# Value context laid out by the host: six tiles of 125 keys and one transfer per chunk, in a cross-attention and mixture-of-experts kernel

## The chip, the core and the metric

The kernel runs on one core of a Trainium2 chip. The metric is the device time of one launch in microseconds, the median of the runs shown. A core has TensorE (matmuls), VectorE (DVE), ScalarE (ACT), GpSimd (POOL) and SyncE (SP), which here issues nearly all transfers, and sixteen DMA engines that carry them out.

## What is computed

x is 8 x 224 x 2048 in float32, the context ctx_4096 is 8 x 750 x 2048. The first half is attention, in which the context is key and value at once, the second a feed-forward layer with a low-rank top-2 mixture of sixteen experts. Cut to what matters here:

```python
def _L0_xattn_ref(query, key):
    a = jnp.einsum('bqd,bkd->bqk', query, key)
    e = jax.nn.softmax(a, axis=-1)
    c = jnp.einsum('bqk,bkd->bqd', e, key)
    return c

x = x + _L0_xattn_ref(_layernorm(x, axis=-1), ctx_4096)
x = x + _L0_ffn_ref(_layernorm(x, axis=-1), base_w, base_b, A, B, router_w)
```

## The kernel before

Each float32 product is made of three matmuls: an operand is split into a high part, converted by ACT, and a low part, which DVE makes by subtraction, and high x high, high x low and low x high are added in PSUM.

The attention half goes through the eight batches one after another (`one(b, stage)` on every engine). A batch has two phases on TensorE.

*Scores.* Queries stand as the stationary operand, two tiles (q) of QT = 112 columns. The context comes transposed (`ctxT`, laid out by the host), in eight pairs j of two 128-row blocks, 750 KB each, into LR = 4 slots. ACT's `ctx_high` (L1045) and DVE's `ctx_low` (L1287) split a pair; lines 789 to 791 multiply. Step j of the scores ends when its pair has been used; SP may load pair j + 4 then (`score_done`).

*Values.* The exponentials (`prob`) are transposed on TensorE (`exps_T`, L884), NT = 6 tiles of keys. Then `outputs_of` (L906 to 908) goes through CH = 4 chunks of 512 columns and, in each, the six tiles t. The keys of a tile are the contraction, so a tile has as many partitions as keys: 128 five times (FULL), then REST = 110. ACT's `value_high` (L1067) and DVE's `value_low` (L1297) split a tile. A chunk c is loaded by `load_raw` (L522, L524), one transfer for the five full tiles, one for the rest, both counted on `raw_loaded[c]`; its buffer is loaded again for the next batch (`raw_again`) when TensorE has used the chunk (`val_used`).

SP's queue is written out by hand in `one` of the sync block. For a batch b in the middle it issues: the late store of x2 of batch b - 1; ctxT pairs 4 to 7, each behind score step j - 4; value chunk 3; ctxT pairs 0 to 3 of batch b + 1 behind score steps 4 to 7; x rows and xT of batch b + 1; value chunk 0 of b + 1; the stores of xT and hn of batch b - 1; value chunks 1 and 2; the early store of x2. In the first batch chunks 0 to 3 are loaded between its own ctxT pairs, in the order ctxT 0 to 3, chunk 0, ctxT 4, x rows, ctxT 5, chunk 1, ctxT 6 and 7, chunk 2, ar, chunk 3, x rows of batch 1. All these transfers go through one queue of SP (q1 in the profile), which has a lane on each of the sixteen DMA engines. DVE takes the statistics of the next batch's x rows in between values 4 to 7 (`row_stats`), in program order.

Behind the eight batches comes the expert half: base weights, routing, expert rows and output tiles (L937 to 939 and others).

Of the kernel before, what the change touches and what calls it, by code (L numbers as in the profile page):

```python
# [24 lines left out]
F32 = mybir.dt.float32  # L25
# [4 lines left out]
P = 128  # L30
BANK = 512
# [6 lines left out]
def as_f32(ap):  # L38

    return ap.bitcast(F32)  # L40
# [29 lines left out]

def xattn_ffn_kernel(nc, x, ctx, bias, ctxT, xT, arT, wT, bT, out):
    NB, LQ, D = x.shape
    LK = ctx.shape[1]
    E, R = bT.shape[0], bT.shape[1]
    QT = LQ // 2
    NQ = 2
    KD = D // P
    NT = -(-LK // P)
    FULL = LK // P
    REST = LK - FULL * P  # L80
    CH = D // BANK
    RE = R + E
    assert LQ == NQ * QT and D == CH * BANK and RE <= P and 2 * R == P


    T = NB * LQ
# [57 lines left out]
    out = out.rearrange("b s d -> (b s) d")  # L144
# [59 lines left out]
    with ExitStack() as stack:  # L204
        def sb(name, shape, dt=F32, of=stack):
            return of.enter_context(nc.sbuf_tensor(name, shape, dt))
# [17 lines left out]
        ident = sb("ident", [P, P])  # L224
# [28 lines left out]
        NR = 4  # L253
        with ExitStack() as first:
            xn = sb("xn", [QT, NQ, D], F32, first)
            ctxT_l, ctxT_in = sb_in("ctxT", [P, LR, CP, LK], first)
            ctxT_h = [sb(f"ctxT_h{i}", [P, CP, LK], F32R, first) for i in range(HR)]
            prob = sb("prob", [QT, NQ, NT * P], F32, first)
            raw, raw_in = sb_in("raw", [P, CH, NT, BANK], first)
            val_h = sb("val_h", [P, NR, BANK], F32R, first)  # L260
            eT_h = sb("eT_h", [P, NQ, NT, QT], F32R, first)
            eT_l = sb("eT_l", [P, NQ, NT, QT], F32R, first)
            at_x2 = [nc.sbuf_base]
            x2 = sb("x2", [QT, NQ, D], F32, first)
# [14 lines left out]
        rows = [xn, x2]  # L279
# [5 lines left out]
        for i in range(AR):  # L285
# [3 lines left out]
            low_part, loaded = sb_in(f"a{i}", [P, KD, P], stack)  # L289
# [76 lines left out]
        consts_ready = sem("consts_ready")  # L366
# [6 lines left out]
        raw_loaded = [sem(f"raw_loaded{c}") for c in range(CH)]  # L373
# [93 lines left out]
        def xT_count(batches):  # L467
            return 16 * sum(len(pieces_of(b)) for b in range(batches))

        def rows_of(t):  # L470
            return P if t < FULL else REST

        X2T_TAIL_AT = (3, 6, 9, 12)
        HID_TAIL_AT, HN_TAIL_AT = 1, 6
        HR_AT, ROUTE_AT, COUNT_AT, PLACE_AT, SCATTER_AT = 3, 4, 6, 6, (6, 7, 8, 9)
# [42 lines left out]
        @block.sync  # L518
        def _(sp):
            def load_raw(b, c):  # L520
                cols = slice(c * BANK, (c + 1) * BANK)
                sp.dma_start(raw_in[:, c, 0:FULL, :],  # L522
                             ctx[b, 0:FULL * P, cols].rearrange("(t p) d -> p t d", p=P)).then_inc(raw_loaded[c], 16)
                sp.dma_start(raw_in[0:REST, c, FULL, :], ctx[b, FULL * P:LK, cols]).then_inc(raw_loaded[c], 16)  # L524

            def load_ctxT(b, j):
                sp.dma_start(ctxT_in[:, j % LR, :, :], ctxT[b, j]).then_inc(ctx_loaded[j % LR], 16)
# [248 lines left out]
        def _(pe):  # L776
# [100 lines left out]
            def exps_T(stage, b):  # L877
                for q in range(NQ):
                    pe.wait_ge(exp_done, b * NQ + q + 1)
                    take(job_no(stage, b, "eT", q))  # L880
                    slot = slot_of(stage, "eT", q)
                    for t in range(NT):
                        at = (t // 3) * BANK + (t % 3) * QT
                        last = pe.transpose(work[:, slot, at:at + QT],  # L884
                                            prob[:, q, t * P:(t + 1) * P], ident[0:QT, 0:QT])
                    last.then_inc(filled, 1)

            def outputs_of(stage, b):

                pe.wait_ge(drained, job_no(stage, b, "eT", NQ - 1) + 1)  # L890
                for e in range(CH * NT):
                    c, t = e // NT, e % NT
                    if stage != "first" and e == HN_AT:
                        hidden_back(stage, b)
                    if stage != "last" and e == SPREAD_AT:
                        spread_mean(stage, b)
                    if t == 0 and c >= 2:

                        pe.wait_ge(x2_done, b * (NQ * CH) + NQ * (c - 1))
                    pe.wait_ge(val_ready, b * (CH * NT) + e + 1)  # L900
                    for q in range(NQ):
                        out = scores[0:QT, (c + 1) % 2, q * BANK:(q + 1) * BANK]
                        used = rows_of(t)
                        eh, el = eT_h[0:used, q, t, :], eT_l[0:used, q, t, :]
                        vh, vl = val_h[0:used, e % NR, :], raw[0:used, c, t, :]
                        pe.matmul(out, eh, vh, start=(t == 0), stop=False)  # L906
                        pe.matmul(out, eh, vl, start=False, stop=False)  # L907
                        last = pe.matmul(out, el, vh, start=False, stop=(t == NT - 1))  # L908
                    last.then_inc(val_used, 1)
# [124 lines left out]
        def _(act):  # L1034
            def high(stage, b, name, n, out, cols, width):

                act.wait_ge(filled, job_no(stage, b, name, n) + 1)
                src = place(stage, name, n).rearrange("p (k c) -> p k c", k=cols)[:, :, 0:width]
                act.activation(out, src, ACT.Copy).then_inc(high_done, 1)

            def ctx_high(b, j):
# [19 lines left out]
            def value_high(b, e):  # L1061
                at_least(act, val_used, b * (CH * NT) + e - NR + 1)
                c, t = e // NT, e % NT
                if t == 0:
                    act.wait_ge(raw_loaded[c], b * 32 + 32)
                used = rows_of(t)
                act.activation(val_h[0:used, e % NR, :], raw_in[0:used, c, t, :],  # L1067
                               ACT.Copy).then_inc(val_high, 1)

            def exponentials(b, q):  # L1070
# [18 lines left out]
            def one(b, stage):  # L1089
# [29 lines left out]
                    high(stage, b, "x2T", NX - 1, four_blocks(nT_h, NX - 1), 2, 2 * LQ)  # L1119
                exponentials(b, 1)  # L1120
                for q in range(NQ):
                    high(stage, b, "eT", q, eT_h[:, q, :, :].rearrange("p (k i) c -> p k (i c)", k=2), 2, 3 * QT)
                for e in range(NR, CH * NT):
                    value_high(b, e)
                    if stage == "first" and e == AR_AT:
# [152 lines left out]
        def _(dve):  # L1278
            def low(stage, b, name, n, high_part, low_part, cols, width):

                dve.wait_ge(high_done, act_no(stage, b, name, n) + 1)
                src = place(stage, name, n).rearrange("p (k c) -> p k c", k=cols)[:, :, 0:width]
                dve.tensor_tensor(low_part, src, as_f32(high_part), ALU.subtract).then_inc(drained, 1)  # L1283

            def ctx_low(b, j):
# [7 lines left out]
            def value_low(b, e):  # L1293
                c, t = e // NT, e % NT
                dve.wait_ge(val_high, b * (CH * NT) + e + 1)
                used = rows_of(t)
                dve.tensor_tensor(raw[0:used, c, t, :], raw_in[0:used, c, t, :], as_f32(val_h[0:used, e % NR, :]),  # L1297
                                  ALU.subtract).then_inc(val_ready, 1)

            def stats(tile, st, sem_stat, i):  # L1300
# [145 lines left out]
            def run_route(lo, hi):  # L1446

                steps = route_steps()
                assert len(steps) == COUNTED
                if lo == 0:  # L1450
                    dve.wait_ge(hr_loaded, 16)
                    dve.wait_ge(row_ids, 2)
                    dve.wait_ge(consts_ready, 1 + E)
                for n in range(lo, hi):
                    if n > 0:
                        dve.wait_ge(route, n)
                    if n == 2:
                        dve.wait_ge(rexp_done, 1)
                    steps[n]().then_inc(route, 1)
# [39 lines left out]
            def one(b, stage):  # L1499
# [41 lines left out]
                if old:  # L1541
                    x2T_low(NX - 1)
                for q in range(NQ):
                    three = lambda tile: tile[:, q, :, :].rearrange("p (k i) c -> p k (i c)", k=2)
                    low(stage, b, "eT", q, three(eT_h), three(eT_l), 2, 3 * QT)
                if old:
                    hidden_out(stage, b)
# [111 lines left out]
                dve.tensor_copy(y_out[:, s % 3, c * BANK:(c + 1) * BANK], y_bank(c)).then_inc(y_right, 1)  # L1659

            dve.memset(part_of_D[:, :], 1.0 / D).then_inc(part_ready, 1)
            dve.memset(prob[:, :, LK:NT * P], 0.0).then_inc(consts_ready, 1)
            for e in range(E):
                dve.memset(rank[:, e:e + 1], float(E - e)).then_inc(consts_ready, 1)
            for n in range(NX):
# [16 lines left out]
            ctx_low(0, 1)  # L1682
            first_low_part(1)
            first_centre(2)
            dve.wait_ge(consts_ready, 1 + E)
            one(0, "first")
            for b in range(1, NB - 1):
                one(b, "mid")
# [251 lines left out]
```

## Time and profile before

| | us |
|---|---|
| median of 3 runs | 1351.94 |
| lowest and highest | 1350.43, 1354.08 |
| the profiled execution | 1354.39 |
| its span (first to last instruction) | 1352.6 |
| TensorE busy | 1327.3 |
| DVE, ACT, POOL busy | 974.7, 601.2, 322.5 |
| granted clock, mean of the span | 0.996 |

Busy times are sums over the span and overlap. Times within the profile count from the span's start. Line numbers are those of the kernel before.

### The profile page before, as it was taken

What the parts mean: (1) busy time and instruction counts of PE and PEld (TensorE: products, weight loads), DVE (VectorE), ACT (ScalarE), POOL (GpSimd) and SP (SyncE); (2) the same over time, 40 slices, a digit from 0 to 9 for tenths busy, and PEclk for the clock granted to TensorE, in tenths of its full rate; (3) what the DMA queues carried; (4) which work ended last, traced back from release to release, by engine and by line L of the source; (5) the groups of instructions that cost most, each with busy time, mean ns of one, the idle gap of its engine ahead of it and who ended that gap; (6) DMA issues with size and microseconds to landing.
All of it is one profiled execution on the core that took longest, in us unless ns stands there. A gap on an engine that the chain in (4) does not pass through costs nothing.

```text
span 1352.6 us, 16784 instructions
## 1 busy us (share of the span) xinstructions
PE 1327.3 (98%) x6543; PEld 1081.0 (80%) x6543; DVE 974.7 (72%) x1254; ACT 601.2 (44%) x768; POOL 322.5 (24%) x229
## 2 busy tenths in 40 slices
PE   7799999999999999999999999999999999999998
PEld 5578788887878788887888888888788888888887
DVE  5698888889798888879475467777677555465554
ACT  3356554645546464546321367877686211111110
POOL 0003012130302112120615723354442111111110
PEclk9899999999999999999999999999999999999999
DMA  9976968878796977769657598999995977878775
GB/s 326 315 258 215 294 242 242 269 251 271 227 304 212 287 259 248 246 227 194 201 161 211 176 296 288 321 324 310 315 250 192 322 255 242 281 250 263 253 260 164
DMA packets 159359, 345.67 MB, mean 256 GB/s; under 512 B 51696, under 2 KB 68080, under 8 KB 145520
## 3 DMA queue, kind: packets, MB, share of 16 engines
q1 hardware_dynamic: 140688, 277.06, 64.5%
q0 software_dynamic: 10528, 52.85, 12.6%
q10 hardware_dynamic: 8064, 14.68, 3.1%
q8 instruction: 52, 0.85, 0.3%
q14 instruction: 27, 0.22, 0.0%
HBM read 260.87 MB, written 99.41 MB: 266 GB/s over the span
## 4 chain that ended last, share of the span: by engine, by line
PE 75%; DVE 12%; DMA 5%; ACT 3%; POOL 3%; issue 2%; SPq 0%; DVEq 0%; POOLq 0%; ACTq 0%
PE scores L937 12%; PE scores L939 12%; PE scores L938 12%; PE scores L906 6%; PE scores L908 6%; PE scores L907 6%; PE scores L789 4%; PE scores L791 3%; PE scores L790 3%; DVE ctxT_l L1287 3%; PE work L973 2%; PE work L974 2%; DMA y_scratch<-y_out,yrow_i 2%; DVE raw_l L1297 2%; POOL hs_scratch L1830 2%
## 5 line engine op out<-in xcount | busy, mean ns | idle before, releaser
L937 PE MATMUL scores<-w_h,a_h 128*128 128x512 f32 x896 | 352.0, 393 | 0.0
L939 PE MATMUL scores<-w_h,a_l 128*128 128x512 f32 x896 | 350.9, 392 | 0.0
L938 PE MATMUL scores<-w_l,a_h 128*128 128x512 f32 x896 | 350.6, 391 | 0.0
L1159 ACT ACTIVATE a_h<-a_in 128x512 fp32r<-128x512 f32 x148 | 83.6, 622 | 313.4 <-DMA a_in<-xT_scratch 211.3
L939 PEld LDWEIGHTS scores<-w_h,a_l 128*128 128x128 f32 x896 | 168.4, 188 | 37.5
L937 PEld LDWEIGHTS scores<-w_h,a_h 128*128 128x128 f32 x896 | 168.3, 188 | 37.5 <-DVE w_l L1584 0.3
L938 PEld LDWEIGHTS scores<-w_l,a_h 128*128 128x128 f32 x896 | 168.5, 188 | 37.1
L1593 DVE TENSOR_TENSOR a_l<-a_in,a_h 128x512 fp32r<-128x512 f32 x148 | 106.0, 763 | 115.3 <-ACT a_h L1159 111.8
L789 PE MATMUL scores<-ctxT_h,nT_h 128*112 128x494 f32 (+1 forms) x512 | 174.3, 340 | 7.8 <-DVE nT_l L1485 7.2
L1067 ACT ACTIVATE val_h<-raw_in 128x512 fp32r<-128x512 f32 x192 | 120.2, 629 | 127.6 <-PE scores L908 127.6
L791 PE MATMUL scores<-ctxT_h,nT_l 128*112 128x494 f32 (+1 forms) x512 | 171.5, 335 | 0.0
L790 PE MATMUL scores<-ctxT_l,nT_h 128*112 128x494 f32 (+1 forms) x512 | 171.4, 335 | 0.0
L1297 DVE TENSOR_TENSOR raw_l<-raw_in,val_h 128x512 fp32r<-128x512 f32 x192 | 153.3, 824 | 22.9 <-ACT val_h L1067 22.6
L906 PE MATMUL scores<-val_h,eT_h 128*112 128x512 f32 (+1 forms) x384 | 154.7, 403 | 3.4 <-DVE eT_l L1283 1.7
L907 PE MATMUL scores<-raw_l,eT_h 128*112 128x512 f32 (+1 forms) x384 | 152.2, 396 | 0.0
L908 PE MATMUL scores<-val_h,eT_l 128*112 128x512 f32 (+1 forms) x384 | 152.1, 396 | 0.0
L1772 POOL TENSOR_TENSOR rs<-ve,mhalf 112x2 f32<-112x2 f32 x16 | 39.4, 2463 | 404.4 <-DVE ve L1310 404.4
L1045 ACT ACTIVATE ctxT_h<-ctxT_in 128x1500 fp32r<-128x1500 f32 x63 | 90.8, 1452 | 96.2 <-PE scores L791 87.7
L1287 DVE TENSOR_TENSOR ctxT_l<-ctxT_in,ctxT_h 128x1500 fp32r<-128x1500 f32 x63 | 107.6, 1717 | 35.6 <-ACT ctxT_h L1045 35.6
L1797 POOL TENSOR_TENSOR res<-res,bias_b 128x512 f32<-128x512 f32 x42 | 63.9, 1523 | 288.6 <-DMA res<-x_scratch 264.6
L1651 DVE TENSOR_TENSOR b_hl<-b_in,b_hl 64x2048 fp32r<-64x2048 f32 x43 | 99.3, 2312 | 43.3 <-ACT b_hl L1175 43.0
L789 PEld LDWEIGHTS scores<-ctxT_h,nT_h 128*112 128x112 f32 x512 | 90.1, 176 | 23.9 <-DVE nT_l L1485 8.5
(168 smaller groups left out, 1936.6 us busy)
## 6 DMA issues: line engine op xcount, KB each, us to landing
ctxT_in<-in_ctxT_dram SPq DMA_DIRECT2D x63, 750.0 KB, 4.7
raw_in<-in_ctx_dram SPq DMA_DIRECT2D x32, 1280.0 KB
a_in<-xT_scratch SPq DMA_DIRECT2D x37, 1024.0 KB
w_in<-in_wT_dram SPq DMA_DIRECT2D x32, 512.0 KB, 6.7
y_add<-y_scratch SPq DMA_DIRECT2D x56, 256.0 KB, 6.2
late_y<-y_scratch SPq DMA_DIRECT2D x56, 256.0 KB, 6.0
nT_in<-in_xT_dram SPq DMA_DIRECT2D x7, 1792.0 KB, 10.1
res<-x_scratch SPq DMA_DIRECT2D x42, 256.0 KB
```

The lines of the kernel that those rows point to most:

```text
L789: pe.matmul(out, qh, ch, start=(k == 0), stop=False)
L790: pe.matmul(out, qh, cl, start=False, stop=False)
L791: last = pe.matmul(out, ql, ch, start=False, stop=(k == KD - 1))
L906: pe.matmul(out, eh, vh, start=(t == 0), stop=False)
L907: pe.matmul(out, eh, vl, start=False, stop=False)
L908: last = pe.matmul(out, el, vh, start=False, stop=(t == NT - 1))
L937: pe.matmul(o, ah, wh, start=(k == 0), stop=False)
L938: pe.matmul(o, ah, wl, start=False, stop=False)
L939: last = pe.matmul(o, al, wh, start=False, stop=(k == KD - 1))
L1067: act.activation(val_h[0:used, e % NR, :], raw_in[0:used, c, t, :], ACT.Copy).then_inc(val_high, 1)
L1287: dve.tensor_tensor(ctxT_l[:, j % LR, :, :], ctxT_in[:, j % LR, :, :], as_f32(ctxT_h[j % HR][:, :, :]), ALU.subtract).then_inc(ctx_ready, 1)
L1297: dve.tensor_tensor(raw[0:used, c, t, :], raw_in[0:used, c, t, :], as_f32(val_h[0:used, e % NR, :]), ALU.subtract).then_inc(val_ready, 1)
```

## The change

The host cuts the values' context into `[batch, chunk, key within tile, tile, 512]` with 750 = 6 x 125. A partition of a chunk then reads 6 x 512 floats, 12 KB in one piece, from the first 125 partitions' rows, and a chunk is one transfer. FULL, REST and `rows_of` go; tiles, conversions, transposes and matmuls of the values have KT = 125 rows. `prob` shrinks from 768 to 750 columns, and the memset of its padding goes. The semaphore of a chunk counts 16 a batch instead of 32.

```diff
@@ -70,17 +70,16 @@
-    LK = ctx.shape[1]
+    LK = ctxT.shape[-1]
...
-    FULL = LK // P
-    REST = LK - FULL * P
+    KT = LK // NT
...
-            prob = sb("prob", [QT, NQ, NT * P], F32, first)
+            prob = sb("prob", [QT, NQ, LK], F32, first)
...
             def load_raw(b, c):
-                cols = slice(c * BANK, (c + 1) * BANK)
-                sp.dma_start(raw_in[:, c, 0:FULL, :],
-                             ctx[b, 0:FULL * P, cols].rearrange("(t p) d -> p t d", p=P)).then_inc(raw_loaded[c], 16)
-                sp.dma_start(raw_in[0:REST, c, FULL, :], ctx[b, FULL * P:LK, cols]).then_inc(raw_loaded[c], 16)
+                sp.dma_start(raw_in[0:KT, c, :, :], ctx[b, c]).then_inc(raw_loaded[c], 16)
...
-                        last = pe.transpose(work[:, slot, at:at + QT],
-                                            prob[:, q, t * P:(t + 1) * P], ident[0:QT, 0:QT])
+                        last = pe.transpose(work[0:KT, slot, at:at + QT],
+                                            prob[:, q, t * KT:(t + 1) * KT], ident[0:QT, 0:QT])
...
-                        used = rows_of(t)
-                        eh, el = eT_h[0:used, q, t, :], eT_l[0:used, q, t, :]
-                        vh, vl = val_h[0:used, e % NR, :], raw[0:used, c, t, :]
+                        eh, el = eT_h[0:KT, q, t, :], eT_l[0:KT, q, t, :]
+                        vh, vl = val_h[0:KT, e % NR, :], raw[0:KT, c, t, :]
...
                 if t == 0:
-                    act.wait_ge(raw_loaded[c], b * 32 + 32)
-                used = rows_of(t)
-                act.activation(val_h[0:used, e % NR, :], raw_in[0:used, c, t, :],
+                    act.wait_ge(raw_loaded[c], b * 16 + 16)
+                act.activation(val_h[0:KT, e % NR, :], raw_in[0:KT, c, t, :],
                                ACT.Copy).then_inc(val_high, 1)
...
-            dve.memset(prob[:, :, LK:NT * P], 0.0).then_inc(consts_ready, 1)
...
+    laid["ctx_4096"] = ctx.reshape(nb, -(-lk // 128), -1, d // 512, 512).transpose(0, 3, 2, 1, 4)
```

SP's queue in batch 1, from the load of xT to the first stores, before (a row names line, operation, target<-source and the shape):

```order
L549 DMA nT_in<-in_xT_dram 128x3584
L522 DMA raw_in<-in_ctx_dram 128x5x512
L524 DMA raw_in<-in_ctx_dram 110x512
L616 DMA xT_scratch<-xT_st 128x16x128
L616 DMA xT_scratch<-xT_st 128x16x96
L621 DMA hn_scratch<-hn 112x2x80
```

and the same place now:

```order
L542 DMA nT_in<-in_xT_dram 128x3584
L517 DMA raw_in<-in_ctx_dram 125x3072
L609 DMA xT_scratch<-xT_st 128x16x128
L609 DMA xT_scratch<-xT_st 128x16x96
L614 DMA hn_scratch<-hn 112x2x80
```

Two transfers have become one at the same place in the queue; nothing else has moved, on SP or on another engine.

## Rows read from the trace of the kernel before

**Rows 1.** The page: busy time of the engines; the SP queue's packets, MB, share.
```profile
PE 1327.3 (98%) x6543; PEld 1081.0 (80%) x6543; DVE 974.7 (72%) x1254; ACT 601.2 (44%) x768; POOL 322.5 (24%) x229
...
q1 hardware_dynamic: 140688, 277.06, 64.5%
```
**Rows 2.** Windows, two middle batches; columns as in the first line.
```profile
core 0: us, PE busy (x) PEld busy (x) DVE busy (x) ACT busy (x) POOL busy (x), PEclk, DMA share, GB/s
...
182.70:259.40 76.70, 76.62 (x433) 62.70 (x432) 66.10 (x85) 40.41 (x48) 14.23 (x7) 1.00 0.81 259
...
413.40:490.10 76.70, 76.57 (x434) 62.92 (x433) 66.25 (x87) 40.39 (x48) 14.39 (x7) 1.00 0.78 259
```
**Rows 3.** DMA view, 573 to 583 us: packets, queue, issues.
```profile
DMA packets 923, 2.33 MB, mean 233 GB/s; under 512 B 43, under 2 KB 43, under 8 KB 921
...
q1 hardware_dynamic: 921, 2.30, 68.0%
...
raw_in<-in_ctx_dram SPq DMA_DIRECT2D x1, 1280.0 KB
ctxT_in<-in_ctxT_dram SPq DMA_DIRECT2D x1, 750.0 KB, 4.4
raw_in<-in_ctx_dram SPq DMA_DIRECT2D x1, 220.0 KB
```
**Rows 4.** Groups by form: value matmuls, value conversions, weight load of the transposes.
```profile
L906 PE MATMUL scores<-val_h,eT_h 128*112 128x512 f32 x320 | 129.4, 404 | 2.7 <-DVE eT_l L1283 1.7 <-DVE raw_l L1297 0.7
...
L1067 ACT ACTIVATE val_h<-raw_in 128x512 fp32r<-128x512 f32 x160 | 100.0, 629 | 108.7 <-PE scores L908 108.7
...
L906 PE MATMUL scores<-val_h,eT_h 110*112 110x512 f32 x64 | 25.3, 395 | 0.7 <-DVE raw_l L1297 0.7
...
L1067 ACT ACTIVATE val_h<-raw_in 110x512 fp32r<-110x512 f32 x32 | 20.2, 632 | 18.9 <-PE scores L908 18.9
...
L884 PEld LDWEIGHTS work<-ident,prob 112*128 112x128 f32 x96 | 9.6, 140 | 2.0 <-ACT prob L1072 2.0
```
**Rows 5.** DMA view, 1 to 40 us, in 40 slices.
```profile
GB/s 40 158 368 423 415 404 403 412 434 418 425 419 418 382 388 386 389 296 91 166 425 413 235 260 252 277 353 233 240 400 368 372 386 394 291 249 362 384 387 391
...
q1 hardware_dynamic: 3799, 13.15, 97.2%
```
**Rows 6.** SP in order of time; the queue's bytes and share, 454 to 480 us.
```profile
454.44 0.47 SPq L524 DMA_DIRECT2D raw_in<-in_ctx_dram  x1
454.96 6.60 SPq L616 DMA_DIRECT2D xT_scratch<-xT_st  x2
...
q1 hardware_dynamic: 6888, 7.65, 91.2%
```
**Rows 7.** Tile ctxT_in, 480 to 500 us: conversions, issue to landing.
```profile
L1045 ACT ACTIVATE ctxT_h<-ctxT_in x4: 1456/1456/1461, 483.5 to 496.2; 128x1500 fp32r<-128x1500 f32 x4
L1287 DVE TENSOR_TENSOR ctxT_l<-ctxT_in,ctxT_h x4: 1714/1718/1722, 485.0 to 497.7; 128x1500 fp32r<-128x1500 f32 x4
...
DMA to landing us min/median/max: 4.3/4.4/5.4
```
**Rows 8.** TensorE and ACT in order of time, the loop's two ends.
```profile
453.82 0.40 PE L906 MATMUL scores<-val_h,eT_h 128*112 128x512 f32 x1
...
496.24 1.46 ACT L1045 ACTIVATE ctxT_h<-ctxT_in 128x1500 fp32r<-128x1500 f32 x1 [0.56 <-PE scores L791]
```
**Rows 9.** First batch: the chain's wait for ctxT; DVE's wait for x rows.
```profile
26.61 13.12 DMA ctxT_in<-in_ctxT_dram
...
64.35 1.29 DVE L1302 BATCH_NORM_STATS2 st<-x 112x6 f32<-112x512 f32 x2 [2.11 <-DMA x<-in_x_dram]
```
**Rows 10.** Windows, first batch: busy time, then granted clock (columns of rows 2).
```profile
33.00:57.00 24.00, 16.49 (x95) 13.17 (x94) 17.24 (x26) 10.80 (x15) 1.64 (x1) 0.99 1.04 308
57.00:63.50 6.50, 5.54 (x13) 4.06 (x14) 1.55 (x2) 0.69 (x3) 0.00 (x0) 0.50 1.00 283
```

More of the change, by code:

```diff
@@ L78, in xattn_ffn_kernel @@
     NT = -(-LK // P)
-    FULL = LK // P
-    REST = LK - FULL * P
+    KT = LK // NT
     CH = D // BANK
     RE = R + E
-    assert LQ == NQ * QT and D == CH * BANK and RE <= P and 2 * R == P
+    assert LK == NT * KT and LQ == NQ * QT and D == CH * BANK and RE <= P and 2 * R == P
     T = NB * LQ
@@ L468, in xT_count @@
             return 16 * sum(len(pieces_of(b)) for b in range(batches))
-        def rows_of(t):
-            return P if t < FULL else REST
         X2T_TAIL_AT = (3, 6, 9, 12)
@@ L1037, in high @@
                 act.wait_ge(filled, job_no(stage, b, name, n) + 1)
-                src = place(stage, name, n).rearrange("p (k c) -> p k c", k=cols)[:, :, 0:width]
+                rows = out.shape[0]
+                src = place(stage, name, n)[0:rows, :].rearrange("p (k c) -> p k c", k=cols)[:, :, 0:width]
                 act.activation(out, src, ACT.Copy).then_inc(high_done, 1)
@@ L1121, in one @@
                 for q in range(NQ):
-                    high(stage, b, "eT", q, eT_h[:, q, :, :].rearrange("p (k i) c -> p k (i c)", k=2), 2, 3 * QT)
+                    high(stage, b, "eT", q, eT_h[0:KT, q, :, :].rearrange("p (k i) c -> p k (i c)", k=2), 2, 3 * QT)
                 for e in range(NR, CH * NT):
@@ L1281, in low @@
                 dve.wait_ge(high_done, act_no(stage, b, name, n) + 1)
-                src = place(stage, name, n).rearrange("p (k c) -> p k c", k=cols)[:, :, 0:width]
+                rows = low_part.shape[0]
+                src = place(stage, name, n)[0:rows, :].rearrange("p (k c) -> p k c", k=cols)[:, :, 0:width]
                 dve.tensor_tensor(low_part, src, as_f32(high_part), ALU.subtract).then_inc(drained, 1)
@@ L1295, in value_low @@
                 dve.wait_ge(val_high, b * (CH * NT) + e + 1)
-                used = rows_of(t)
-                dve.tensor_tensor(raw[0:used, c, t, :], raw_in[0:used, c, t, :], as_f32(val_h[0:used, e % NR, :]),
+                dve.tensor_tensor(raw[0:KT, c, t, :], raw_in[0:KT, c, t, :], as_f32(val_h[0:KT, e % NR, :]),
                                   ALU.subtract).then_inc(val_ready, 1)
@@ L1452, in run_route @@
                     dve.wait_ge(row_ids, 2)
-                    dve.wait_ge(consts_ready, 1 + E)
+                    dve.wait_ge(consts_ready, E)
                 for n in range(lo, hi):
@@ L1543, in one @@
                 for q in range(NQ):
-                    three = lambda tile: tile[:, q, :, :].rearrange("p (k i) c -> p k (i c)", k=2)
+                    three = lambda tile: tile[0:KT, q, :, :].rearrange("p (k i) c -> p k (i c)", k=2)
                     low(stage, b, "eT", q, three(eT_h), three(eT_l), 2, 3 * QT)
@@ L1684, in _ @@
             first_centre(2)
-            dve.wait_ge(consts_ready, 1 + E)
+            dve.wait_ge(consts_ready, E)
             one(0, "first")
```

## The prediction

> **What bounds the kernel now.** I read the page's busy line first: TensorE is busy 98% of the span, and the SP queue's transfers take 64.5% of the sixteen DMA engines [rows 1]. Then the windows cut at batch borders: a batch of the attention half takes 76.7 us, TensorE is busy all of it, and the DMA engines stand at 0.78 to 0.81 [rows 2]. So TensorE sets the pace and the DMA has a fifth to spare, as long as the bytes lie evenly on the sixteen engines. The expert half, behind the eight batches, has none of the edited lines.
>
> **How a transfer is spread.** This decides everything, and one short window shows it. Between 573 and 583 us three transfers run: the 128-partition part of a value chunk (640 rows of 2 KB), its 110-partition rest (110 rows), and one ctxT pair (128 rows). That makes 878 data packets; the SP queue shows 921, so 43 small ones are left, and 43 is also the count under 512 B [rows 3]. If every transfer ended with one small packet on each of sixteen engines there would be 48. 43 is 16 + 16 + 11: the 110-partition transfer used eleven engines, ten partitions each. 110 does not divide by 16, and 11 is its largest factor up to 16. The new transfer has 125 partitions on both sides; 125 is 5 x 5 x 5, so the same division gives **five engines with 25 partitions each**. The Trainium skill (DMA: Bandwidth & Descriptors, Why a DMA increments its semaphore by 16 and not by 1) says that a transfer takes the largest number of engines up to 16 that divides the slowest dimension of both sides; this trace agrees with its 11. By that rule the sum is the one below; by an even spread it would be about nothing.
>
> **The change part by part.**
> Instruction shapes: values with 125 rows in place of 128 and 110. The two old forms cost the same: 404 against 395 ns a matmul, 629 against 632 ns a conversion on ACT [rows 4]; counts don't change. 0 us. The transposes of the exponentials load 125 columns in place of 128: 96 loads of about 0.14 us, by a fortieth less [rows 4], under 1 us. The removed memset on DVE runs while the first load is under way: 0. One transfer fewer per chunk takes 0.47 us off SP thirty-two times [rows 6], but SP waits for TensorE between its issues, so 0; if it did not, 15 us would be the most, and no row shows TensorE waiting for SP. Fewer, larger packets: bytes are the same, a gain I take as 0 (below).
>
> The five engines: a chunk is 125 x 12 KB = 1.536 MB. Before, each engine carried 96 KB of it; now five carry 307 KB. Price: with all sixteen busy and large packets, slices of the start-up run at 403 to 434 GB/s [rows 5], which is 25 to 27 GB/s for one engine; over the mixed first 39 us it is 13.15 MB at 97.2% busy, 21.7 GB/s for one engine [rows 5]. So a chunk takes 11.4 to 14.2 us on those five. I take 25 GB/s, **12.3 us**, because only five engines will then ask HBM. Before, it was 3.8 us by the same rate. Everything else on the queue also has a sixteenth on each of these five engines, and each engine works in order, so all later transfers wait for them.
>
> Middle batches. Follow the loop from "chunk 0 of batch b used" (the first matmul of chunk 1, 453.82 us) to "scores step 4 of batch b+1" (496.3 us, when ACT and SP have just had the end of step 3, 496.24) [rows 6, 8]: 42.5 us. On the queue stand in this order: values 0, stores of xT, hn, values 1, values 2, the early x2 store, the late one, and ctxT pair 4. Between 454 and 480 the queue moves 7.65 MB in 91.2% of 26 us, 23.7 us [rows 6]. Of these bytes 4.61 MB are three value chunks, 11.5 us at 25 GB/s an engine; so the rest takes 12.2 us. After the change: 0.6 us to issue, 3 x 12.3 = 36.9, 12.2 for the rest, 1.1 for the late store (448 KB), 4.4 from issue to landing for ctxT pair 4 [rows 7], then its conversion, 1.46 on ACT and 1.72 on DVE [rows 7]: 58.4 us. Step 4 can't start before that: **+16 us** in each of batches 2 to 7, 96 us. In batch 1 no xT store stands in the loop (1.8 MB at 12.2 us for 3.04 MB, 7.4 us): +8 us.
>
> As a check, a middle batch now has 0.78 x 76.7 = 60 us of work per engine [rows 2]; take out 4 x 3.8 and put in 4 x 12.3, and a slow engine has 94 us, close to the 92.7 of the loop. Both limits say the same.
>
> First batch. DMA is the bound here already: the last ctxT pair is waited for until 39.7 us [rows 9], and the x rows of batch 1 are waited for by DVE's statistics until 64.35 [rows 9]. Ahead of those x rows four value chunks now stand, 1229 KB instead of 384 KB on a slow engine, 34 us more at 25 GB/s; before, all that stood ahead was 18.5 MB (xT 1.8, ctxT 6.1, four chunks 6.1, x rows 3.7, ar 0.7) in about 62 us, 21 of them by bytes the chunks' and 41 the rest's. Now the chunks take 4 x 12.3 = 49 and the rest 38 to 41, being relieved while eleven engines idle. I take **+25 us**, since DVE hands out the values behind those statistics and TensorE follows it; the ends are +13 (only the last ctxT pair counts: 422 KB more ahead of it, 17 us, less 4 of relief) and +34 (no relief at all).
>
> TensorE's clock. In the first batch TensorE was busy 16.5 of 24 us, then the granted clock fell to 0.50 for 57 to 63.5 us [rows 10], that is 1.2 in place of 2.4 GHz, about 3.3 us lost. A stall of 16 us is a deeper pause. I charge it for six batches: +20 us; the other end is 0.
>
> Sum: 96 + 8 + 25 + 20 = +149 us. The profiled execution took 1354.4 us (span 1352.6), 2.4 above the median of the three runs, 1351.9. So 1503, against the median 1501; **1500 us**.
>
> **The rivals.**
> 1. *Even spread* (not slower). The value transfer is divided over all sixteen engines in spite of 125, because the contiguous side is cut elsewhere. Then a chunk takes what it takes now, six packets of 2 KB a partition become one of 12 KB, and only the first batch can gain, being bound by DMA: two chunks of 3.8 us stand ahead of the last ctxT pair; if larger packets took a tenth off them, 0.8 us. Time 1351. It decides if the small packets of the new transfer number sixteen. Against it: the eleven of the 110-partition part [rows 3]. Chance 0.07. The change would not do what it does by my rule; it is also the case in which one transfer for two is a plain saving.
> 2. *Five engines, but hidden.* The loop has slack I did not see, or five engines alone run faster than 27 GB/s each, which no row can show since all sixteen were always busy together. At 35 GB/s a chunk takes 8.8 us: the loop is 58.4 - 10.5 = 47.9, +5 us a batch, 32 for six, nothing in batch 1, +10 in the first: 1394. For it: TensorE's loads of ctxT have four slots. Against: the start-up slices, with nothing but large packets, stay at 434 GB/s or below [rows 5]. Chance 0.05.
> 3. *Five engines at the mixed rate.* 14.2 us a chunk, since the 25-partition shares collide with each other or with the stores: +5.7 us in each loop, 34 for six, 4 in batch 1, 8 in the first: 1546. Chance 0.2.
> 4. *Forecast*, 12 us a chunk, with or without the clock's loss: 1448 (11.4 us a chunk, 16 us less; no clock loss, 20 less; the other transfers relieved by 2 us a loop, 12; 4 in the first batch) to 1525. Chance 0.66. The last 0.02 is for a split on one engine, 61 us a chunk and far over 2000 us in all.
>
> **How the numbers follow.** The likeliest case gives 1500. The range takes in cases 3 and 4 with their bounds, 1435 to 1560, and leaves out most of 1, 2 and the split on one engine, 0.14, and something for terms missed. A change under 0.3% (4 us) can't be told from none here. Faster by more than that: 0.02, only if rival 1 gains more than I can find; within 0.3%: 0.05; slower: 0.93.
>
> **What would show it.** In a window that holds one value transfer and one ctxT pair: 125 + 128 data packets and 5 + 16 small ones. Each middle batch 93 to 96 us, with one pause of TensorE of about 16 us before scores step 4, released by DMA of ctxT_in through ACT and DVE; mean DMA share over sixteen engines lower than 0.78 although the queue is the bound; a granted clock of 0.50 for some us behind each pause. From the first matmul of the expert half to the end the time should be unchanged. Wrong if batches still take 76.7 us, or if the value transfer shows sixteen small packets; a sum too large if the clock stays at 1.00 or if pauses fall in other places as well as there.

## The result and the profile after

| | us |
|---|---|
| before, median of 5 runs | 1352.98 (1350.43 to 1357.36) |
| changed, median of 5 runs | 1529.85 (1528.69 to 1532.91) |
| ratio, 95% interval | 1.1311 (1.1284 to 1.1338) |
| profiled execution, its span | 1529.7, 1528.0 |

The change makes the kernel 13% slower. 1529.85 lies in the range of 1435 to 1560; the predicted 1500 was 30 too low, so +149 was forecast and +177 came.

The page of the changed kernel, busy line, SP queue, and the group of the scores' first matmul (out<-in, count | busy, mean ns | idle before, releaser):

```profile
PE 1347.2 (88%) x6543; PEld 1098.6 (72%) x6543; DVE 976.6 (64%) x1253; ACT 600.3 (39%) x768; POOL 330.6 (22%) x229
...
q1 hardware_dynamic: 119984, 277.06, 58.8%
...
L782 PE MATMUL scores<-ctxT_h,nT_h 128*112 128x494 f32 (+1 forms) x512 | 183.8, 359 | 146.7 <-DVE ctxT_l L1280 123.2
...
L898 PE MATMUL scores<-val_h,eT_h 125*112 125x512 f32 x384 | 155.3, 404 | 21.2 <-DVE raw_l L1289 18.9
...
ctxT_in<-in_ctxT_dram SPq DMA_DIRECT2D x63, 750.0 KB, 19.5
```

and the last of them in the profile before:

```profile
ctxT_in<-in_ctxT_dram SPq DMA_DIRECT2D x63, 750.0 KB, 4.7
```

TensorE went from 98% to 88% [rows 1]; its idle time stands before the scores and hangs on ctxT, whose loads take 19.5 us from issue to landing (median; 4.7 before) although nobody edited them. The value matmul on 125 rows costs 404 ns, as the 128-row form did [rows 4].

The packet count says how the transfers were spread. The queue went from 140688 packets [rows 1] to 119984, 20704 fewer, at the same 277.06 MB. Data packets: 32 chunks of 125 instead of 750, 20000 fewer. The other 704 are small ones, 22 a chunk: 16 + 11 = 27 before, so 5 now. **Five engines**, as the eleven of the old 110-partition part [rows 3] had suggested. The Trainium skill (DMA: Bandwidth & Descriptors, Why a DMA increments its semaphore by 16 and not by 1) gives the same number for 125; here rows and rule agree at 110 and at 125.

Two windows of ten microseconds, DMA view. In the first, 118 to 128 us, value chunks alone move (packets of 12 KB and four small ones). In the second, 348 to 358 us, only 35 of the packets are of a value chunk; the others are what stands behind chunk 2, x2 stores and ctxT:

```profile
DMA packets 113, 1.34 MB, mean 134 GB/s; under 512 B 4, under 2 KB 4, under 8 KB 4
...
q1 hardware_dynamic: 113, 1.34, 31.7%
```

```profile
DMA packets 243, 1.30 MB, mean 130 GB/s; under 512 B 18, under 2 KB 18, under 8 KB 208
...
q1 hardware_dynamic: 243, 1.30, 31.3%
```

Five sixteenths are 31.25%: in both, five engines are busy without a break and eleven have nothing, at 26 to 27 GB/s each. In the second, TensorE waits: eleven engines have finished their shares of the ctxT pair and five have not. Chain, SP in order of time, and windows of that pause and behind it:

```profile
330.01 28.41 DMA ctxT_in<-in_ctxT_dram
358.51 1.46 ACT ctxT_h L1038
359.99 1.73 DVE ctxT_l L1280
...
398.72 0.29 SPq L517 DMA_DIRECT2D raw_in<-in_ctx_dram  x1
399.06 16.01 SPq L609 DMA_DIRECT2D xT_scratch<-xT_st  x3
...
342.70:361.80 19.10, 0.00 (x1) 0.00 (x0) 1.81 (x2) 3.29 (x2) 0.00 (x0) 0.58 0.44 146
361.80:366.30 4.50, 4.44 (x14) 3.73 (x15) 2.79 (x3) 4.32 (x4) 0.00 (x0) 0.50 0.34 142
```

ctxT pair 4 is 28.4 us under way, then comes its conversion, as in the prediction's loop; TensorE is idle for 19 us, and for 4.5 us of work behind it the granted clock is 0.50 (columns of [rows 2]). SP's issue of three xT stores takes 16.0 us, 13.0 of them for the second store alone (5.6 in the profile before). Three of them in the profile before, SP in order of time:

```profile
531.62 8.38 SPq L616 DMA_DIRECT2D xT_scratch<-xT_st  x3
```

SP itself is held twice as long. That it waits for room on the five slow engines is my reading; no view shows how full an engine's lane is.

By batch (windows cut where the scores of a batch begin; columns of [rows 2]), some rows of before and of the changed kernel:

```profile
0.00:94.40 94.40, 77.86 (x358) 59.73 (x359) 68.98 (x118) 40.76 (x53) 4.50 (x16) 0.96 0.92 307
94.40:171.70 77.30, 77.08 (x433) 62.77 (x432) 66.22 (x86) 40.41 (x48) 14.41 (x6) 1.00 0.78 255
634.40:1352.60 718.20, 711.84 (x3164) 581.88 (x3162) 442.96 (x544) 274.51 (x373) 218.64 (x172) 1.00 0.80 254
```

```profile
0.00:135.60 135.60, 86.05 (x358) 66.08 (x359) 69.10 (x117) 40.70 (x53) 4.48 (x16) 0.82 0.67 199
135.60:230.90 95.30, 79.64 (x433) 64.40 (x432) 66.25 (x86) 40.31 (x48) 14.40 (x6) 0.91 0.65 204
325.70:424.50 98.80, 79.40 (x433) 64.61 (x432) 66.25 (x85) 40.31 (x48) 14.33 (x6) 0.90 0.65 202
815.10:1528.00 712.90, 707.81 (x3164) 581.62 (x3162) 444.36 (x544) 274.30 (x373) 226.81 (x172) 1.00 0.80 255
```

The first batch lost 41.2 us, batch 1 18.0, batches 2 to 7 together 121.5 (584.2 against 462.7), the expert half got 5.3 shorter. In a middle batch the mean DMA share *fell*, from 0.78 to 0.81 [rows 2] to 0.65, while the DMA became the bound: a mean over sixteen engines hides five full ones.

The account further down needs one more thing: how long a packet took. From the packet records of the traces, the mean of the value chunks' 12 KB packets; in the kernel before, 12 KB go as six packets of 2 KB, 100 ns each:

| kernel | first batch, ns | batches 2 to 7, ns |
|---|---|---|
| before, six packets of 2 KB | 600 | 600 |
| changed, five engines | 642 | 565 |
| 112 + 13 partitions | 757 | 761 |
| padded to 128, one transfer | 472 | 549 |
| padded, 112 + 16 | 800 | 763 |
| 100 + 25 partitions | 828 | 673 |

The last four kernels are experiments below. In batches 2 to 7 of the changed kernel, chunks 0 to 3 have 504, 506, 704 and 546 ns. 25 packets an engine make that 12.6, 12.6, 17.6 and 13.7 us a chunk. Chunk 2 is the dearest, and its slow packets fall together with work on the other engines: from 332 to 347 us, while these took their shares of ctxT pairs 4 to 7, its packets had 778 ns on average, and from 348 to 351 us, alone, 463.

### The profile page after: what moved, and what is told of

Read it like the earlier page. It is cut to its first block, busy times and chain, and to the rows that moved or that the text cites. A ratio compares the mean times of both kernels' runs of the same rounds, so it can differ in the third digit from the quotient of the medians.

```text
span 1528.0 us, 16751 instructions
## 1 busy us (share of the span) xinstructions
PE 1347.2 (88%) x6543; PEld 1098.6 (72%) x6543; DVE 976.6 (64%) x1253; ACT 600.3 (39%) x768; POOL 330.6 (22%) x229
## 3 DMA queue, kind: packets, MB, share of 16 engines
q1 hardware_dynamic: 119984, 277.06, 58.8%
## 4 chain that ended last, share of the span: by engine, by line
PE 70%; DMA 17%; DVE 6%; POOL 2%; another core or an unknown queue 1%; issue 1%; ACT 1%; SPq 0%; DVEq 0%; ACTq 0%; POOLq 0%
DMA ctxT_in<-in_ctxT_dram 14%; PE scores L929 12%; PE scores L931 12%; PE scores L930 11%; PE scores L898 5%; PE scores L900 5%; PE scores L899 5%; PE scores L782 4%; PE scores L784 4%; PE scores L783 4%; PE work L965 3%; PE work L966 3%; DMA xn<-in_x_dram 2%; POOL hs_scratch L1821 2%; PE work L834 2%
## 5 line engine op out<-in xcount | busy, mean ns | idle before, releaser
L782 PE MATMUL scores<-ctxT_h,nT_h 128*112 128x494 f32 (+1 forms) x512 | 183.8, 359 | 146.7 <-DVE ctxT_l L1280 123.2
L782 PEld LDWEIGHTS scores<-ctxT_h,nT_h 128*112 128x112 f32 x512 | 96.1, 188 | 165.3 <-issue 124.5
L784 PE MATMUL scores<-ctxT_h,nT_l 128*112 128x494 f32 (+1 forms) x512 | 179.2, 350 | 0.0
L783 PE MATMUL scores<-ctxT_l,nT_h 128*112 128x494 f32 (+1 forms) x512 | 179.1, 350 | 0.0
L1059 ACT ACTIVATE val_h<-raw_in 125x512 fp32r<-125x512 f32 x192 | 120.1, 629 | 147.6 <-PE scores L900 147.6
L898 PE MATMUL scores<-val_h,eT_h 125*112 125x512 f32 x384 | 155.3, 404 | 21.2 <-DVE raw_l L1289 18.9
L1289 DVE TENSOR_TENSOR raw_l<-raw_in,val_h 125x512 fp32r<-125x512 f32 x192 | 153.1, 824 | 23.2 <-ACT val_h L1059 23.1
L899 PE MATMUL scores<-raw_l,eT_h 125*112 125x512 f32 x384 | 152.7, 398 | 0.0
L900 PE MATMUL scores<-val_h,eT_l 125*112 125x512 f32 x384 | 152.6, 397 | 0.0
L1779 POOL TENSOR_TENSOR xT_st<-nT_h,nT_l 128x896 f32<-128x896 f32 x32 | 72.5, 2272 | 270.7 <-DVE nT_l L1276 270.7
## 6 DMA issues: line engine op xcount, KB each, us to landing
ctxT_in<-in_ctxT_dram SPq DMA_DIRECT2D x63, 750.0 KB, 19.5
```

Source lines behind the costliest of these rows:

```text
L782: pe.matmul(out, qh, ch, start=(k == 0), stop=False)
L783: pe.matmul(out, qh, cl, start=False, stop=False)
L784: last = pe.matmul(out, ql, ch, start=False, stop=(k == KD - 1))
L1059: act.activation(val_h[0:KT, e % NR, :], raw_in[0:KT, c, t, :], ACT.Copy).then_inc(val_high, 1)
L1289: dve.tensor_tensor(raw[0:KT, c, t, :], raw_in[0:KT, c, t, :], as_f32(val_h[0:KT, e % NR, :]), ALU.subtract).then_inc(val_ready, 1)
```

## The experiments

**The spread against the layout.** The change does two things at once, a new host layout with large packets and a transfer of 125 partitions. Three kernels part them. First, the changed kernel with each chunk cut so that it divides:

```diff
-                sp.dma_start(raw_in[0:KT, c, :, :], ctx[b, c]).then_inc(raw_loaded[c], 16)
+                for lo, hi in ((0, 112), (112, KT)):
+                    sp.dma_start(raw_in[lo:hi, c, :, :], ctx[b, c, lo:hi]).then_inc(raw_loaded[c], 16)
```

> The changed kernel with each value chunk loaded by two transfers, partitions 0 to 111 and 112 to 124, layout of the host kept. Theory A (the spread over five engines is the whole cause): 112 divides by 16, 13 partitions go to thirteen engines, so the most loaded engine carries 8 rows of 12 KB instead of 25; 1345 to 1356 us, middle batches 76.7 us, 29 small packets (16 + 13) per chunk. Theory B (the host layout, the 12 KB packets or the 125-row tiles cost the time, the spread little): 1480 us or more. Theory C (half and half): in between, around 1440.

Measured: 1360.69 us, ratio to the kernel before 1.0067 (1.0041 to 1.0093). The spread is nearly the whole cause; of the 0.7% that is left, the part beyond 1356 us was not expected, and it gets its own experiment below. Second, the host pads a chunk to 128 rows and one transfer carries it:

```diff
+    laid["ctx_4096"] = _np.pad(laid["ctx_4096"], ((0, 0), (0, 0), (0, 3), (0, 0), (0, 0)))
...
-                sp.dma_start(raw_in[0:KT, c, :, :], ctx[b, c]).then_inc(raw_loaded[c], 16)
+                sp.dma_start(raw_in[:, c, :, :], ctx[b, c]).then_inc(raw_loaded[c], 16)
```

> The changed kernel with the host's chunk padded by three rows of zeros to 128 partitions; one transfer of 128 partitions per chunk, 2.4% more bytes in it; everything else as in the change. Theory A (spread): 16 engines, 8 rows each, as in the split kernel, 1345 to 1356 us. Theory B (one large transfer with 12 KB packets is slow in itself): like the change, 1480 us or more.

Measured: 1353.28 us, ratio 1.0008 (0.9991 to 1.0024). With three rows of zeros the layout, the single transfer and the 12 KB packets cost no time, and gain none either: 12 KB take 549 ns of an engine instead of 600, but TensorE sets the pace of a middle batch. Third, the old layout and tiles with the spread made bad:

```diff
-                sp.dma_start(raw_in[:, c, 0:FULL, :],
-                             ctx[b, 0:FULL * P, cols].rearrange("(t p) d -> p t d", p=P)).then_inc(raw_loaded[c], 16)
+                full = ctx[b, 0:FULL * P, cols].rearrange("(t p) d -> p t d", p=P)
+                for lo, hi in ((0, 125), (125, P)):
+                    sp.dma_start(raw_in[lo:hi, c, 0:FULL, :], full[lo:hi]).then_inc(raw_loaded[c], 16)
```

> The kernel before, its layout and its tiles of 128 and 110 keys kept, but the transfer of the five full tiles cut into partitions 0 to 124 and 125 to 127: 625 packets of 2 KB on five engines, 15 on three, 110 on eleven. Theory A (spread alone): most loaded engine carries about 125 + 5 + 10 packets of 2 KB per chunk, 287 KB against 307 in the change, so nearly all of the loss comes back: 1490 to 1525 us, a stall of 14 to 19 us before scores step 4 of every batch from 1 on. Theory B (layout or packet size): 1350 to 1360.

Measured: 1500.2 us, ratio 1.1086 (1.1056 to 1.1116). The page of this kernel, SP queue:

```profile
q1 hardware_dynamic: 140432, 277.06, 58.4%
```

256 packets fewer than before, 8 a chunk: 16 small ones became 5 + 3. So 125 goes to five engines with 2 KB packets too, and this alone, without layout, packet size or tiles of 125, brings 147 of the 177 us. The 30 us between them have no experiment: the fullest engine carries 287 KB a chunk instead of 307, and this kernel's chain also passes through SP (7% of its span, 0% in the changed kernel), at the issue of a value transfer for one:

```profile
311.12 9.26 SPq L524
```

**A smaller dose.** 100 partitions on ten engines and 25 on five leave 15 rows on the fullest engine:

```diff
+                for lo, hi in ((0, 100), (100, KT)):
+                    sp.dma_start(raw_in[lo:hi, c, :, :], ctx[b, c, lo:hi]).then_inc(raw_loaded[c], 16)
```

> The changed kernel with each chunk cut into partitions 0 to 99 (ten engines, ten rows each) and 100 to 124 (five engines, five rows each): the most loaded engine carries 15 rows of 12 KB, 184 KB, 7.4 us, instead of 25 rows. Loop theory (a batch is late only by what the loop from chunk 0 used to scores step 4 exceeds its 42.5 us): 63 us measured with 12.3 us a chunk, less 3 x 4.9 = 48, so +5 us or so in batches 2 to 7, less in batch 1, and about +14 in the first batch: 1390 to 1405 us. Proportional theory (loss in proportion to the rows above eight, 7 of 17): 1352 + 0.41 x 177 = 1425 us. Theory with room in the loop: 1355 to 1370.

Measured: 1446.11 us, ratio 1.0686 (1.0642 to 1.073): above all three theories, nearest to the proportional one. The packets are 15 more a chunk than the data ones, 10 + 5, as the division says. Windows of its first batch and of batches 2 to 7 together, and the longest and shortest of the chain's six waits for ctxT pair 4:

```profile
0.00:130.10 130.10, 84.11 (x359) 64.77 (x360) 69.18 (x117) 40.54 (x53) 4.47 (x16) 0.86 0.81 216
...
210.00:734.10 524.10, 473.62 (x2591) 387.36 (x2590) 396.75 (x507) 244.96 (x294) 84.92 (x35) 0.95 0.74 221
```

```profile
300.38 22.00 DMA ctxT_in<-in_ctxT_dram
...
562.98 13.15 DMA ctxT_in<-in_ctxT_dram
```

The first batch loses 35.7 us, nearly as much as with five engines. The other six lose 524.1 - 462.7 = 61.4 together, 10 each. The loop with 4.9 us taken off each of three chunks is 58.4 - 14.7 = 43.7 us, one more than the 42.5 that are free; yet the wait for ctxT pair 4 is still there in every batch. The loop names the right wait and the wrong price. The 12 KB packets of chunks 0 to 2 took 675, 710 and 715 ns here, 31.5 us for fifteen of each, where 3 x 7.4 = 22.1 were reckoned. With this price, and 9.5 us for the other transfers (worked out under *Middle batches* below), the same loop gives 50.3 us, an estimate of +8 a batch: TensorE's six pauses before step 4 are 8 us on average, and the rest of the 10 stands beside them. A row doesn't cost the same in every spread.

**Which chunks matter.** `cuts_of` chooses one transfer (five engines) or 112 + 13 partitions:

```diff
+        def cuts_of(b, c):
+            return [(0, KT)] if c < CH - 1 else [(0, 112), (112, KT)]
```

> Chunks 0, 1 and 2 in one transfer (five engines), chunk 3 in two (112 and 13 partitions, even). Loop theory (chunks 0 to 2 stand between the use of chunk 0 and scores step 4, chunk 3 does not): middle batches stay at 95 to 98 us as in the change, the first batch is 10 us shorter: 1505 to 1522 us. Load theory (what counts is the work of a slow engine in a whole batch, 60 us before and 8.5 us more for each five-engine chunk): 60 + 25.5 = 85.5 us a batch, +9 us over 76.7 instead of +20: 1440 to 1460 us.

Measured: 1543.32 us, ratio 1.1395 (1.1309 to 1.148). With `c == CH - 1`, only chunk 3 on five engines:

> Only chunk 3 in one transfer on five engines, chunks 0 to 2 even. Loop theory: it is issued behind scores step 3 and needed 50 us later, middle batches 76.7 us; only the first batch loses up to 10 us, since the x rows of batch 1 stand behind it: 1352 to 1366 us. Proportional theory (a quarter of the loss): 1352 + 177 / 4 = 1396 us.

Measured: 1427.98 us, ratio 1.0543 (1.0455 to 1.0632). Both theories fell, in both runs. Relieving chunk 3 gains nothing beside the other three, and chunk 3 alone costs 76 us, more than a quarter of 177. All these kernels load their even chunks as 112 + 13, which itself costs some 8 us (1360.69 above), so a few us of each excess are the cut's. With chunk 3 alone, a middle batch in the windows view:

```profile
203.10:289.10 86.00, 78.50 (x434) 64.08 (x433) 66.16 (x85) 40.45 (x48) 14.34 (x6) 0.96 0.83 225
```

And its chain of waits in the batch behind it:

```profile
325.66 18.93 DMA xn<-in_x_dram
344.66 0.57 issue
345.23 0.68 DVE st L1298
345.90 0.60 DVE raw_l L1293
```

The x rows of the next batch, issued 19 us behind chunk 3, land 18.9 us after their issue instead of some 10; DVE stands at the statistics between values 4 and 5 and the values behind it are late. That is a second gate, about 20 us behind the first, which the prediction had only in the first batch. So I moved chunk 3's load behind those x rows and ctxT pair 3 of the next batch:

```diff
-                if not first:
+                if last:
                     raw_again(b - 1, CH - 1)
...
                     load_ctxT(b + 1, LR - 1)
+                    if not first:
+                        raw_again(b - 1, CH - 1)
```

> Only chunk 3 on five engines, as in the run that took 1428 us, but issued behind the x rows and the last ctxT pair of the next batch (batches 1 to 6). Theory: there the 7 us pause at values 5 came from DVE waiting for x rows that stood behind chunk 3. Then batches 1 to 6 go back to 77 us, the first stays at 104 and the total is 1370 to 1376 us. Rival (the load as such is too much): the pause moves to another wait and the total stays at 1420 or more.

Measured: 1452.99 us, ratio 1.074 (1.0704 to 1.0777), 25 us worse. The wait for x rows is gone, and the chain has another:

```profile
341.04 28.92 DMA nT_in<-in_xT_dram
370.04 0.40 DVE bias_b L1329
```

The rival was right: xT is now the transfer behind chunk 3, and DVE waits for it. The same edit with chunks 0 to 2 on five engines and chunk 3 even:

> Chunks 0 to 2 on five engines, chunk 3 even, as in the run that took 1543 us, but chunk 3 of batches 1 to 6 is issued behind the last ctxT pair of the next batch instead of ahead of them. Interference theory (the even chunk 3 runs on the eleven free engines while the slow five finish chunk 2, and slows them): the pauses before scores step 4 shrink from 19 to 24 us to 15 to 18, total 1505 to 1525 us. Without interference the order of chunk 3 can't matter for ctxT pair 4, issued ahead of it in either case: 1540 us or more.

Measured: 1564.21 us, ratio 1.1562 (1.1523 to 1.1602), 21 us worse instead of 18 to 38 better. So the even chunk 3 is not what makes that kernel slower than the change, or the later place costs more than it gives: it stands now before xT and chunk 0. Why 1543 is more than 1530 stays open; its six pauses before step 4 are 20.8 us on average against 18.1 in the changed kernel, and the ratios' intervals overlap. What these four runs show is that neither of the two places tried for chunk 3 has room for a chunk of five engines: what stands behind it becomes late, whether ctxT, x rows or xT.

**Do the parts add?** Only batch 0 on five engines (`b == 0`):

> Only the four chunks of batch 0 on five engines, all later ones even. If the parts add: the first batch's 41 us over the kernel before, nothing else, the expert half as before: 1385 to 1400 us. If the first batch's lateness is partly taken up again by the later batches (SP and the queue being ahead then): 1365 to 1385.

Measured: 1395.22 us, ratio 1.0301 (1.0224 to 1.0379). Windows of its first and second batch:

```profile
0.00:135.80 135.80, 86.35 (x359) 65.70 (x360) 69.10 (x117) 40.60 (x53) 4.48 (x16) 0.84 0.76 210
135.80:214.50 78.70, 77.76 (x433) 62.73 (x432) 66.20 (x86) 40.43 (x48) 14.40 (x6) 1.00 0.86 248
```

And only the later ones (`b > 0`):

> Batch 0's chunks even, all later ones on five engines. If the parts add: 1530 - 41 = 1489, within 1480 to 1500 us, batch 1 longer by what its own loop gives. My prediction's step gave batch 1 only +8 us; the change showed +18. If the 10 us more are left over from the first batch's backlog, batch 1 shows 85 us here and the total is near 1480; if they are its own, 95 us and 1489.

Measured: 1502.38 us (1495.38 and 1509.38; the profile is of the longer one), ratio 1.1093 (1.0945 to 1.1241). Its batch 1:

```profile
108.00:207.40 99.40, 79.18 (x434) 64.56 (x432) 66.27 (x85) 40.32 (x48) 14.41 (x6) 0.90 0.60 191
```

The first batch loses 41.4 us by itself and leaves nothing behind: batch 1 is within 2 us of its old time. Batch 1 on five engines takes 99.4 us even behind an even batch 0. So most of its loss is its own and not a backlog. The parts sum to 43 + 150 = 193 against 177 measured. Of the 16 us too many, the first batch of the kernel with the later ones has 13.6: it takes 108.0 us although its own chunks are even. The kernel cut at 112 everywhere has 98.5, so about 4 of them are the cut's; the rest is not explained, and the two runs of this kernel are 14 us apart.

**The 0.7% of the cut at 112.** Each engine carries eight rows with 112 + 13 as with 128. The padded kernel cut at 112 has the same eight rows, data packets and engines as the uncut one, and 16 small packets a chunk more:

```diff
+                for lo, hi in ((0, 112), (112, P)):
+                    sp.dma_start(raw_in[lo:hi, c, :, :], ctx[b, c, lo:hi]).then_inc(raw_loaded[c], 16)
```

> The padded kernel (128 partitions, 12 KB each) with each chunk cut into partitions 0 to 111 and 112 to 127. Both cuts go to all sixteen engines, 7 rows and 1 row, so every engine carries the same eight rows as in the padded kernel; only which partitions an engine writes is different. Count theory (only the rows per engine matter): 1353 us as there, first batch 81.6 us. Mapping theory (an engine whose share is not the eight partitions that it has in a transfer of 128 gets in the way of the others): the first batch is 3 to 6 us longer, as it is in the kernel cut at 112 (86.1 us), and the total 1356 to 1361 us.

Measured: 1361.99 us, ratio 1.0065 (1.0044 to 1.0085), where the uncut one has 1.0008. The count theory is out; the mapping theory has the direction and somewhat too little. The DMA view over 1 to 40 us, SP queue (packets, MB, share), first the uncut kernel, then the cut one:

```profile
q1 hardware_dynamic: 2444, 13.53, 93.5%
```

```profile
q1 hardware_dynamic: 2193, 11.72, 98.9%
```

The cut kernel moves 13% less at a higher busy share. Windows of the first batch and of batch 2, cut where the scores begin, first the uncut kernel, then the cut one:

```profile
0.00:93.80 93.80, 78.61 (x358) 60.84 (x359) 69.07 (x117) 40.57 (x53) 4.47 (x16) 0.96 0.86 312
172.40:249.30 76.90, 76.80 (x433) 63.02 (x432) 66.16 (x86) 40.44 (x48) 14.33 (x6) 1.00 0.78 254
```

```profile
0.00:103.80 103.80, 83.20 (x358) 63.45 (x359) 69.10 (x117) 40.61 (x53) 4.48 (x16) 0.92 0.97 276
181.40:258.10 76.70, 76.60 (x434) 63.14 (x433) 66.26 (x85) 40.43 (x48) 14.33 (x6) 1.00 0.84 249
```

In batch 2 nearly the same bytes take 0.84 instead of 0.78 of the engines' time, and TensorE hides it. The first batch, bound by DMA, takes 10.0 us more: the whole of the loss.

The packet records say where the time goes: the same 12 KB packets take 763 ns instead of 549 in batches 2 to 7, 800 instead of 472 in the first batch. Eight of them are 1.7 and 2.6 us more a chunk on every engine; the small packets, about 10 ns each, are nothing beside that. Left untested is whether two transfers of large packets would do the same with shares like those of the uncut one; the kernel before, too, has two a chunk, at 0.78 to 0.81 [rows 2].

**A version slightly shorter than both.** In the first batch of the padded kernel chunk 1 goes behind ctxT pairs 6 and 7, and the x rows of batch 1 ahead of chunk 3:

```diff
-                    if first and j == LR + 1:
+                    if first and j == NPC - 1:
                         load_raw(0, 1)
...
-                        load_raw(0, 3)
                         load_row(1)
+                        load_raw(0, 3)
```

> The padded kernel with two loads of the first batch in another order: value chunk 1 behind ctxT pairs 6 and 7, and the x rows of batch 1 ahead of value chunk 3. Each puts 1.57 MB, about 4 us of the full queue, behind something that is waited for. If the first batch is bound by the last ctxT pair and those x rows: 3 to 4 us less, 1349 to 1350 us. If something else bounds it by then: 1353, no change; more than 1355 if chunk 3 is late for its values.

Measured: 1347.23 us, ratio to the kernel before 0.997 (0.9953 to 0.9987), 0.3% shorter. Its first 89.8 us, which is where its batch 1 begins (94.4 before, 93.8 in the padded kernel), in a profile of its shortest run, 1343.99 us:

```profile
0.00:89.80 89.80, 77.34 (x358) 59.95 (x359) 68.97 (x117) 40.57 (x53) 4.47 (x16) 0.98 0.90 326
```

The gain comes with the order, since the padded kernel without it is level with before. No run has this order in the old layout, so what the layout adds to it is not shown.

## Why the prediction was right, and where it was off

*The spread* (five engines from the eleven of 110): right, by the packet count, and shown to be the cause by the padded kernel (+0.1%) and the old layout on five engines (+10.9%). Rival 1, an even spread, is out; so is rival 2, since the five run at 26 to 27 GB/s each when they are alone. Rival 3, 14.2 us a chunk, is nearer to the result with its 1546 (16 off) than the forecast with its 1500 (30 off), and the packets have its price: 571 ns on average over all chunks, 14.3 us.

*Instruction shapes, 0 us*: right. 404 ns a matmul and 629 ns a conversion with 125 rows. The padded kernel has the same tiles and is level with before.

*Middle batches, +16 and 3.3 for the clock, 116 for six*: measured 121.5. The pause before step 4 is released by ctxT pair 4 through ACT and DVE, as the loop says. The six pauses are 16.2 to 19.9 us, 18.1 on average, instead of 16; the clock's part is about 2.3 us rather than 3.3 (4.5 us of work at 0.50 behind the pause; the rest of the half-rate time falls into the pause). The nearness is in part luck, for two terms of the loop were off in opposite directions. Chunks 0 to 2 took 42.9 us by their packets, not 36.9. And the 12.2 us for the other transfers came from pricing the three chunks of the kernel before at 25 GB/s, 11.5 us; by their 2 KB packets in that window, 2250 of 101 ns on sixteen engines, they took 14.2, which leaves 9.5. With both put right the loop gives 61.7 us; measured from chunk 0 used to step 4 it was 59.5 to 61.9. With 184 KB on the fullest engine instead of 307 the loop as written gives +1 a batch, and the batches took 10 more on average; the packets of that kernel bring it to +8 (above). So the step's place and form are confirmed, and its price, one rate for every spread and every neighbour, is what failed.

*Batch 1, +8 us*: mis-sized, measured +18.0. The step was "no xT store stands in the loop", taken as 7.4 us off, which makes the loop 51.0 us. It took 57.2, from chunk 0 used at 110.4 to step 4 at 167.6. The packet records show two parts of the 6.2 between: chunk 0's first packet starts only at 113.0, since the five engines bring ctxT and xT of batch 1 until then, and the three chunks took 40.1 us, not 36.9. A third part lies outside the loop: the clock's 2.3 us were charged for batches 2 to 7 only. The run with only the later batches on five engines gave that batch 99 us behind an even first one, so five-engine chunks of the first batch aren't needed for the loss.

*First batch, +25*: mis-sized, measured 41.2. DVE's wait for the x rows of batch 1 in the changed kernel:

```profile
105.56 1.29 DVE L1294 BATCH_NORM_STATS2 st<-x 112x6 f32<-112x512 f32 x2 [20.90 <-DMA x<-in_x_dram]
```

They come 41.2 us later than before [rows 9], all of the loss. The mis-sized term is the chunks' 4 x 12.3 = 49 us: by their packets (631, 524, 735 and 678 ns) they took 15.8, 13.1, 18.4 and 17.0 us, 64.2 in all. The other 41 of the 105.6 us are what the step had for the rest, 38 to 41, at its upper end: the idle eleven brought no relief. The four chunks don't share the loss evenly. In the kernel with chunk 3 alone on five engines the first batch takes 117.1 us, 22.7 over before. Of the 28 us by which the whole prediction fell short, 16 are here and 10 in batch 1.

*The check by load, 94 us against 92.7*: near the 97 measured on average, and misleading, for two of its readings failed: 524.1 / 6 = 87.4 us a batch at 15 rows (it would give 60 + 4 x 3.6 = 74) and 86 us in batches with chunk 3 alone (60 + 8.5 = 69). A batch is longer well before a slow engine is full, because what is waited for stands behind a chunk.

*The expert half, unchanged*: 712.9 against 718.2 us. The same instructions took between 712.7 and 718.2 us in the profiles of these kernels, so I give the 5 us no cause.

## What to carry to other kernels

Before a layout changes a transfer's partition count, factor the count: 125 means five engines, 110 eleven, 128 or 112 sixteen; pad to 128 rather than save three rows. The profile has a direct check, the number of packets under 512 B in a window, one for each engine that a transfer uses (16, 11, 5, and 10 + 5 here), and a mean DMA share that falls while waits for DMA grow is the other sign. A slow transfer costs most through what stands behind it on the queue, and moving it here only chose who waits. Price a chunk with the packet times of the spread it will have; the single rate of the forecast was 12.3 us a chunk where 14.3 came, and 16 in the first batch.

## What the runs showed of the hardware that was not expected

- Sixteen engines with equal rows aren't enough. 112 + 16 partitions of 12 KB kept the engines busy 0.84 of a middle batch, 128 in one transfer 0.78, at 249 and 254 GB/s; a 12 KB packet took 763 ns against 549, and the first batch took 10 us more. The Trainium skill (SBUF — State Buffer, Door 1: the DMA port swizzle) says that each of sixteen ports of SBUF serves a fixed set of eight partitions, in groups of four; shares of seven or 25 neighbouring partitions would run across such groups. The 763 against 549 ns agree with that, but no run shows a port.
- On five engines a chunk's price depends on its neighbours: 11.8 us (470 ns a packet) for chunks 0 and 1 of batch 1, which run nearly alone, 18.4 us (735 ns) for chunk 2 of the first batch. The slow packets fall together with other transfers on the eleven engines (778 ns beside ctxT, 463 alone); why a neighbour slows them, no run shows.
- SP's issues take long while five engines are behind and eleven are idle for much of the time: one xT store took 13.0 us to issue (5.6 before), and in the first batch four ctxT issues took 7.9, 6.4, 5.2 and 1.8 us, one behind the other:

```profile
56.78 21.54 SPq L520 DMA_DIRECT2D ctxT_in<-in_ctxT_dram  x4
```
